# Attention with relative positions: the tokens' update moved to GpSimd, small steps placed in other units of a batch

## The reference

```
def _forward(src, ...):
    x = _layernorm(src, ln1_g, ln1_b)
    q, k, v = ...                                   # 16 heads of 8
    ac = einsum('bihd,bjhd->bhij', q, k)
    bd = einsum('bihd,phd->bhip', q, p) at distance i - j
    att = softmax((ac + bd) * scale)
    attn_out = einsum('bhij,bjhd->bihd', att, v) @ wo
    src = src + attn_out
    x2 = _layernorm(src, ln2_g, ln2_b)
    sel = sigmoid(x2 @ sel_w);  scores, idx = top_k(sel, 4)
    h = relu(einsum('bsd,edh->bseh', x2, keys))
    return src + einsum('bseh,ehd,bse->bsd', h, values, gate)
x = _layernorm(x);  x = x + 0.5 * _forward(x, ...)  # both times
```

## Time and profile before

| | |
|---|---|
| runs | 2728.84, 2732.15, 2733.09 us; median 2732.15 |
| profiled execution | 2728.11 us, span 2726.4 us, granted clock 0.963 |
| busy in the span | PE 89%, DVE 71%, ACT 58%, POOL 57% |
| attention of `f4` (scores from 839 to 1381 us of the span) | 542 us |
| attention of `f6` (scores from 1927 to 2472 us) | 545 us |

### The profile page before, as it was taken

One profiled execution on the slowest core, in us unless ns is written; L12 is line 12 of the kernel. 1 busy time (PEld: TensorE's weight loads), 2 busy tenths in 40 slices (PEclk: granted clock), 3 DMA queues, 4 the chain that ended last, 5 costly groups with the idle time before them and its releaser, 6 DMA issues. The chain is left out here.

```text
span 2726.4 us, 59982 instructions
## 1 busy us (share of the span) xinstructions
PE 2436.3 (89%) x19038; PEld 1835.0 (67%) x19038; DVE 1929.8 (71%) x5169; ACT 1581.3 (58%) x4641; POOL 1557.1 (57%) x2343
## 2 busy tenths in 40 slices
PE   7999799799977999999988988999799999998898
PEld 5788677578865777777777335665577777777733
DVE  4554388455546899999876456776589999987645
ACT  2332244333326999999930226777699999993022
POOL 4322666332324678888743655554567888874365
PEclk9999899899998999999999997999899999999999
DMA  3720366370005455555455126553445545445512
GB/s 121 311 82 1 74 141 141 120 301 1 1 22 137 124 137 140 137 136 137 130 186 151 46 62 143 114 111 82 105 130 136 137 135 142 137 127 178 158 53 64
DMA packets 302396, 326.64 MB, mean 120 GB/s; under 512 B 31718, under 2 KB 274150, under 8 KB 294902
## 3 DMA queue, kind: packets, MB, share of 16 engines
q1 hardware_dynamic: 252934, 280.83, 37.9%
q0 software_dynamic: 12288, 25.19, 3.3%
q10 hardware_dynamic: 36864, 16.79, 2.1%
HBM read 133.36 MB, written 185.01 MB: 117 GB/s over the span
## 5 line engine op out<-in xcount | busy, mean ns | idle before, releaser
L2073 DVE TENSOR_REDUCE a_nm<-a_sr 128x2 f32<-128x512 f32 x256 | 166.9, 685 | 69.2 <-PE a_sr L1805 68.2
L3207 POOL TENSOR_TENSOR f4o_kv<-a5b_room 128x256 f32<-128x256 f32 x192 | 140.2, 731 | 107.7 <-DVE a5b_room L3075 102.6
L3207 POOL TENSOR_TENSOR f6o_kv<-a5b_room 128x256 f32<-128x256 f32 x192 | 140.3, 731 | 97.6 <-DVE a5b_room L3075 91.8
L2978 ACT ACTIVATE f6a_pr<-f6a_sr,f6a_nm 128x256 f32<-128x256 f32 x384 | 181.4, 486 | 12.0 <-DVE f6a_nm L3063 10.9
L2978 ACT ACTIVATE f4a_pr<-f4a_sr,f4a_nm 128x256 f32<-128x256 f32 x384 | 181.4, 486 | 9.5 <-DVE f4a_nm L3063 7.8
L3075 DVE TENSOR_TENSOR a5b_room<-f4a_ur,f4a_turn 128x512 f32<-128x512 f32 x192 | 131.2, 684 | 44.1 <-PE f4a_ur L2815 43.7
L2837 PE MATMUL f6a_sr<-all_ks,all_qs 96*128 96x256 bf16 x512 | 144.0, 281 | 13.6 <-ACT f6a_pr L2978 10.1
L2837 PE MATMUL f4a_sr<-all_ks,all_qs 96*128 96x256 bf16 x512 | 143.7, 281 | 13.8 <-ACT f4a_pr L2978 10.4
L3075 DVE TENSOR_TENSOR a5b_room<-f6a_ur,f6l_turn 128x512 f32<-128x512 f32 x192 | 131.5, 685 | 34.4 <-PE f6a_ur L2815 33.9
L2854 PE MATMUL f6a_tr<-all_table,f6a_pr 128*128 128x128 f32 x1024 | 154.8, 274 | 0.0
L2854 PE MATMUL f4a_tr<-all_table,f4a_pr 128*128 128x128 f32 x1024 | 154.7, 273 | 0.0
(11 more groups left out here) (672 smaller groups left out, 8481.8 us busy)
## 6 DMA issues: line engine op xcount, KB each, us to landing
slots<-f_zero SPq DMA_DIRECT2D x100, 512.0 KB, 6.1
f4a_slide<-f4o_kv SPq DMA_DIRECT2D x64, 383.0 KB
f6a_slide<-f6o_kv SPq DMA_DIRECT2D x64, 383.0 KB
f4o_kv<-f4a_slide SPq DMA_DIRECT2D x64, 256.0 KB
f6o_kv<-f6a_slide SPq DMA_DIRECT2D x64, 256.0 KB
f4o_src<-slots SPq DMA_DIRECT2D x128, 64.0 KB, 2.2
slots<-f4m_y ACTq DMA_DIRECT2D x128, 64.0 KB, 2.3
f6o_src<-slots SPq DMA_DIRECT2D x128, 64.0 KB, 2.2
```

Of the source, the lines that this page charges most:

```text
L2073: nc.vector.tensor_reduce(nm[:, r // 2, t, at_:at_ + 2], sr[:, g % SB, :].rearrange("p (x s) -> p x s", x=2), AX.X, ALU.max, negate=True). ...
L2978: last = nc.scalar.activation(pr[:, n % 4, x, :], from_, ACT.Exp, bias=nm[:, n % SB, x:x + 1], scale=sign, accum_out=zs[:, b[1], t, h:h + 1])
L3207: nc.gpsimd.tensor_tensor(rr[:, o % RAW, :], tmp[:, o % 2, 0, :], tmp[:, o % 2, 1, :], ALU.add)\
```

## The change

- The update of the tokens on DVE (unit 9, one operation) goes away. POOL does it in unit 11 in two: `half = 0.5 * s1` into a new tile, then `x_b = x_b + half`. Two semaphores are added: `halved` (DVE waits for it before it writes the next `s1`, in unit 6 of the next step) and `x_moved` (POOL, before it writes `half` again).
- On DVE `place_chosen` goes from unit 6 to 2, `place_sum` from 10 to 4, `place_row` from 11 to 5, `gate_one` from 12 to 13, `gate_mask` from 14 to 15, and `gate_sum` from unit 15 to unit 0 of the next step.
- On ACT `opening.normal` goes from unit 9 to 11, `normal_tokens` from 11 to 15, `second_part` from 13 to 12. On PE and ACT `x2t` goes from 12 to 13 and `sel` from 14 to 15.

```
-        AT = {"xt": 8, "qk": 10, "x2t": 12, "sel": 14, "src": 11, "ln": 3}
+        AT = {"xt": 8, "qk": 10, "x2t": 13, "sel": 15, "src": 15, "ln": 3}
@@ scalar, small
-                if n == 13 and b:
+                if n == 12 and b:
                     act.wait_ge(desk.emptied, desk.done(it, "qk"))
                     lead.second_part(act, b[0])
-                if n == 9 and e and kept(e):
+                if n == 11 and e and kept(e):
                     opening.normal(act, e[0])
@@ vector
             GATES = {5: opening.gate_inverse, 6: opening.gate_best, 9: opening.gate_index, 10: opening.gate_number,
-                     12: opening.gate_one, 14: opening.gate_mask}
+                     13: opening.gate_one, 15: opening.gate_mask}
-            PLACES = {6: opening.place_chosen, 9: opening.sum_masks, 10: opening.place_sum,
-                      11: opening.place_row}
+            PLACES = {2: opening.place_chosen, 4: opening.place_sum, 5: opening.place_row,
+                      9: opening.sum_masks}
+                i = it[0] - 4
+                if n == 0 and 0 <= i < B - 1:
+                    dve.wait_ge(desk.emptied, desk.done((it[0] - 1, (it[1] + 1) % 2), "sel"))
+                    opening.gate_sum(dve, i)
                 i = placed(it)
-                    if n == 6:
+                    if n == 2:
                         dve.wait_ge(desk.emptied, desk.done(it, "count"))
                         if i:
                             dve.wait_ge(x2_ready, i * TT)
+                            dve.wait_ge(halved, i)
-                    if n == 9:
-                        nc.vector.scalar_tensor_tensor(x_b[:, i, :, :], s1[:, :, :], 0.5, x_b[:, i, :, :],
-                                                       ALU.mult, ALU.add)
-                    if n == 15 and kept(e):
-                        dve.wait_ge(desk.emptied, desk.done(it, "sel"))
-                        opening.gate_sum(dve, i)
@@ gpsimd, small
+                if e and n == 11:
+                    pool.wait_ge(opening.s1_aggr, e[0] + 1)
+                    if e[0]:
+                        pool.wait_ge(x_moved, e[0])
+                    nc.gpsimd.tensor_scalar(half[:, :, :], s1[:, :, :], 0.5, None, ALU.mult).then_inc(halved, 1)
+                    pool.wait_ge(halved, e[0] + 1)
+                    nc.gpsimd.tensor_tensor(x_b[:, e[0], :, :], x_b[:, e[0], :, :], half[:, :, :], ALU.add).then_inc(x_moved, 1)
```

More of the change, by code:

```diff
@@ L2650, in relative_attention @@
         qs, ks = k.qs, k.ks
-        nm = a.sb("nm", [P, SB, 2])
+        nm, half = a.sb("nm", [P, SB, 2]), a.sb("half", [P, TT, C])
         zs = a.sb("zs", [P, 2, TT, H])
@@ L2667, in relative_attention @@
                      ("sel", 3, B)], 1)
-        AT = {"xt": 8, "qk": 10, "x2t": 12, "sel": 14, "src": 11, "ln": 3}
+        AT = {"xt": 8, "qk": 10, "x2t": 13, "sel": 15, "src": 15, "ln": 3}
         ur_ps, ur_filled, ur_turned, ur_moved = a.ps("ur", [P, 2, 512]), a.sem("ur_filled"), a.sem("ur_turned"), a.sem("ur_moved")
-        nm_ready, av_done, rz_ready, rz8_ready, yn_ready, rr_ready, rr_hi_ready, rr_lo_ready = [a.sem(n) for n in (
-            "nm_ready av_done rz_ready rz8_ready yn_ready rr_ready rr_hi_ready rr_lo_ready").split()]
+        nm_ready, av_done, rz_ready, rz8_ready, yn_ready, rr_ready, rr_hi_ready, rr_lo_ready, x_moved, halved = [a.sem(n) for n in (
+            "nm_ready av_done rz_ready rz8_ready yn_ready rr_ready rr_hi_ready rr_lo_ready x_moved halved").split()]
         free = opening.kv[:, 1, :, :].rearrange("p e c -> p (e c)")
@@ L3084, in move_band @@
                 nc.vector.tensor_copy(band[:, e % 2, 0, :], ur_ps[:, n % 2, 0:BAND]).then_inc(ur_turned, 1)
-            GATES = {5: opening.gate_inverse, 6: opening.gate_best, 9: opening.gate_index, 10: opening.gate_number, 12: opening.gate_one,
-                     14: opening.gate_mask}
+            GATES = {5: opening.gate_inverse, 6: opening.gate_best, 9: opening.gate_index, 10: opening.gate_number, 13: opening.gate_one,
+                     15: opening.gate_mask}
             KEPT = {5: opening.gate_inverse, 6: opening.gate_best, 9: opening.gate_left, 10: opening.gate_kept}
-            PLACES = {6: opening.place_chosen, 9: opening.sum_masks, 10: opening.place_sum,
-                      11: opening.place_row}
+            PLACES = {2: opening.place_chosen, 4: opening.place_sum, 5: opening.place_row,
+                      9: opening.sum_masks}
             def small(it, n):
```

## The result

The changed kernel takes 2813.0 us (median of 4 runs, 2805.1 to 2815.5) against 2732.6 for the kernel before (4 runs): 1.029 times, 95% interval 1.0265 to 1.0315. It is slower, and the prediction had 2718. The profiled execution takes 2810.7 (span 2809.0) against 2728.1.

A forecast was written before the change was run, and what follows sets the result against it. No engine was the bound: three written-out orders hold each other up, and a step loses what ACT waits. Full steps 14.0, plus early steps 1.8, less 1.4 at the ends, gave 14.4 us off 2732.15: 2717.8, range 2706 to 2734.

The forecast's parts named there:

- The update off DVE: Unit 9: removing the update's 1.23 us, with `place_sum` out of unit 10, ends PE's 1.06 us wait for L3084.
- The price of DVE's time in unit 9: From one step: 0.64 us less on DVE in unit 9 gave back 0.45, some 70%.
- The other moves of DVE: Place operations, `gate_mask` and `gate_one` moved into covered or idle time: counted at nothing; without the cover 0.1 to 0.4 each.
- ACT's moves: `normal_tokens` (0.77 us) and `sel` (0.36) leave A; the moved 1.02 lies in time in which ACT waited.
- B: From the end of ACT's unit 14 to the next unit 4's end: 12.27 to 12.70 us, 0.43 more.
- A: From the end of ACT's unit 4 to the end of unit 14: 21.99 to 20.83 us, gaining 1.16.
- the new wait for `qk`: Unit 10: PE ends `qk` at 10.14, ACT asks at 9.74 after its unit 4, a new wait of 0.40 us.
- The last step of each attention: POOL's two operations end about 0.7 us after DVE's last: 0.7 lost per attention (0.5 to 1.7), 1.4 in all.
- `gate_sum` meets the scatter: No-change rival, unit 0: `gate_sum` waits out POOL's scatter, `v` comes 0.74 us later, 2732 remains; chance 0.20.
- POOL too late for unit 0: Slower rival: a 1.75 us multiplication delays POOL, the copy L3142 loses 0.99 a step, 2741 us; chance 0.10.

The follow-up runs named there:

- kernel 4: The kernel before with the update alone moved to GpSimd in unit 11, none of the other moves: 2735.8 us, 1.002.
- kernel 10: The kernel before with the update on GpSimd for all batches and ScalarE's five moves, `gate_sum` in unit 0: 2739.8 us, 1.003.
- kernel 1: The changed kernel with `gate_one` back in unit 12, all else kept: 2755.4 us, 1.009.
- (b): The kernel before with the update on GpSimd except the last batch, plus `sel` in unit 15 and `gate_sum` in unit 0: 2732.5 us.
- (c): The kernel before with the update on GpSimd except the last batch, plus `opening.normal` in unit 11 and `x2t` in 13: 2731.7 us.
- kernel 8: The changed kernel with the last batch's update on VectorE and `sum_masks` alone moved from unit 9 to 10: 2731.2 us, 1.000.
- kernels 2 and 3: First: the kernel before with `gate_one` alone in unit 13, 2727.0 us. Second: the changed kernel with the update back on VectorE, 2743.4 us.

## Why the prediction was wrong

The full steps add up from the runs: 34.45 before; 33.80 with the update on GpSimd (kernel 4); 34.04 with ScalarE's moves (10); 34.66 once `sum_masks` is held up (1); 36.33 once `gate_one` is (step of 1199.58); 37.9 with the clock at half for some 3 us of it.

- **"The update off DVE": right.** It held DVE for 1.23 us and PE's stall of 1.06 was behind it. Alone, taking it away makes PE's wait for L3084 fall from 16.8 us to 5.8 in ten steps, and gives back 0.65 a step. That this is close to the 0.7 forecast is luck, since the forecast had put its gain down to ACT's moves. POOL's multiplication took 0.85 to 0.89 us (0.75 taken), its addition 0.73 (0.726), and in that kernel the steps show no cost of the work queued behind them. (The price of DVE's time in unit 9 was read off a step in which `sum_masks` took 0.47 instead of 0.33: DVE was 0.50 us shorter there, not 0.64, so the share passed on is nearer 90 than 70%.)
- **The step that failed: "The other moves of DVE ... counted at nothing; without the cover, 0.1 to 0.4 each."** `gate_one` was taken to lie in DVE's idle time, at 0.1 to 0.4 if not, without a look at where POOL's run stands in unit 13, and `sum_masks`, which isn't moved, had no term at all. Both read two SBUF tiles. The reason stood in the prediction itself, of the update: "it waits for POOL there". In unit 9 of before `sum_masks` was ahead of POOL's run by 0.2 us only (timeline):

```profile
1063.03 0.33 DVE L2561 TENSOR_TENSOR f4o_mask<-f4o_mask 128x32 bf16<-128x32 bf16 x1
...
1063.23 0.74 POOL L3207 TENSOR_TENSOR f4o_kv<-a5b_room 128x256 f32<-128x256 f32 x1
```

  With the place operations moved that lead went: in kernel 10 with all of ScalarE's moves, `sum_masks` takes 0.33; in kernel 1, which differs from it by the place operations and `gate_mask`, 2.15. Which of these takes the lead away was not tried. So in unit 9 an operation that had escaped the run took the update's place in waiting for it, and the forecast's "L3084 ends before PE is ready" held only without the other moves. Counted at nothing, the two together cost 2.3 us a step.
- **No term for the clock.** PE's stall of 1.86 us was followed in most steps by a granted clock of 0.50, half of full speed (1.2 of 2.4 GHz), for some 3 us: 1.55 us a step. Before, the stall of 1.06 left it at 1.00.
- **"ACT's moves" and "B": a gain of 0.73 forecast, 0.40 measured without the holds.** At the forecast's own cuts, the ends of ACT's last exponential (L2978) of units 4 and 14, the medians of the ten full steps of `f4` are:

  | | A | B | A + B |
  |---|---|---|---|
  | kernel before | 22.18 | 12.26 | 34.44 |
  | update alone (4) | 21.50 | 12.30 | 33.80 |
  | with ACT's five moves (10) | 21.16 | 12.88 | 34.04 |

  A gave back 1.02 of the 1.16, but 0.68 of that comes with the update alone; ACT's departing work, to which the forecast put down nearly all of it, is worth 0.34. B grew by 0.62 and not 0.43, by the wait that was named: with `sel` in unit 15 ACT waits longer for unit 0's maxima (b). So ACT's moves cost 0.25 where they were to bring the gain. The row that (c) adds is that work moved into a unit which still holds other work of ACT makes PE wait (16.0 against 6.4 us); the new wait for `qk`, 0.4 a step, came there as forecast.
- **"The last step of each attention": 0.7 forecast, 8.6 measured.** The working took the barrier's time from a trace in which GpSimd had been idle for 17.45 us, and counted only GpSimd's own two operations.
- **Rivals.** "`gate_sum` meets the scatter" didn't come: its operation takes 0.183 to 0.186 in every step. "POOL too late for unit 0" didn't either: the copy of unit 1 takes 0.63. Slower came by the mechanism of the first, an operation of VectorE held by GpSimd, at two operations that were not examined. The sum had no term for the clock, a far too small one for the ends, and the range reached to neither.

The Trainium skill (SBUF — State Buffer, Who interferes with whom) also says that a VectorE instruction with two SBUF inputs contends with a GpSimd instruction that reads SBUF, and that one with a single input outside the two-port modes doesn't. The runs agree: 2.53 us against 0.42 at the same place. The prediction had weighed only that section's rule on two-port modes, and against `gate_sum` alone. Where the Trainium skill (same section) has issue order decide, the starts in the traces turn at a lead of about 0.15 us and not at nothing: `gate_one`, started 0.13 us first, waited out three instructions of GpSimd.

## What to carry to other kernels

Before an operation of VectorE with two SBUF inputs is moved, or anything ahead of it is, look up in the timeline how far it is ahead of GpSimd's next run: here that lead, not its own duration, set its price, and a lead of 0.2 us was lost by small moves elsewhere. Move one thing at a time: of this change the two parts that gain (the update but for the last batch, and `normal_tokens`) make 0.8%, and the others turned that into a loss of 2.9%. Work given to an engine that was idle at the end of a stage can make it the last at the barrier; here it paid to leave the last batch out.

## What the runs showed of the hardware

- Two VectorE operations with two SBUF inputs, `sum_masks` and `gate_one`, were held when they started up to 0.15 us ahead of a GpSimd arithmetic operation (186 of 187), and not when they started 0.16 to 0.5 us ahead (246 of 247).
- How long such an operation is held differs. It waited out all three of GpSimd's back-to-back instructions (2.15 us for an operation that takes 0.33, 2.53 for one of 0.42), two of them (1.82, kernel 8) or only the rest of the first (0.62, kernels 2 and 3), and where it got in between, GpSimd's next instructions took longer (1.62 instead of some 1.4). What decides where it gets in is not shown.
- Beside a GpSimd scatter VectorE's two-input product of unit 2 (L2567) took 0.276 us a half, its median in the changed kernel.
- The same idle times of TensorE (1.16 and 1.86 us) left the granted clock at 1.00 (2.4 GHz) in one full step of `f4` and took it to 0.50 (1.2 GHz) for some 3 us in the other nine; the rows don't tell what decides.
- GpSimd comes out of the barrier 8.95 to 9.64 us after its last operation when that is the last of all engines; behind an idle GpSimd the barrier took 1.2 us from VectorE's last operation.
